# Opening of the first attention: four units split ahead of the first products, one unit later than before in steps 1 and 2

## What is computed

```python
x = x + tanh(g_xattn[0]) * L0_xattn(layernorm(x), ctx, ctx)   # windowed attention, 16 heads of 16
x = x + tanh(g_ffn[0])   * L0_ffn(layernorm(x), ...)          # top-1 of 16 experts
x = x + tanh(g_xattn[1]) * L1_xattn(layernorm(x), ctx, ctx, mask, wq, wk, wv, ...)  # linear attention
x = x + tanh(g_ffn[1])   * L1_ffn(layernorm(x), ...)          # top-2 of 8 experts
```

## Time and profile before

| what | us |
|---|---|
| median of 3 runs (778.89 to 784.18) | 779.85 |
| the profiled execution, its own time | 787.87 |
| its span in the profile | 786.1 |

### The profile page before, as it was taken

The page is one execution under the profiler, slowest core; times in us unless marked ns, Lnnn a source line. Parts: engine busy times, 40 slices in busy tenths (PEclk is TensorE's granted clock), DMA queues, the critical chain, the costliest instruction groups (busy, mean ns, idle before and its releaser), DMA issues. The chain is left out here.

```text
span 786.1 us, 16260 instructions
## 1 busy us (share of the span) xinstructions
PE 717.5 (91%) x5287; PEld 593.2 (75%) x5287; DVE 372.7 (47%) x1131; ACT 315.2 (40%) x851; POOL 344.2 (44%) x468
## 2 busy tenths in 40 slices
PE   4868999998999999998899976999999999999994
PEld 2435766676666999997666643999999999999994
DVE  3366777887546755444888756122122112212210
ACT  3314666665545333331566520432332233233221
POOL 5123333342116556433378623544554454455322
PEclk9977999999989999999999987999999999999998
DMA  4965666666675999933344447257452442445211
GB/s 142 215 126 105 123 123 123 129 119 123 193 250 188 375 373 374 362 103 123 44 75 62 122 134 255 62 153 220 121 140 52 115 109 47 111 110 152 44 23 15
DMA packets 146935, 114.68 MB, mean 146 GB/s; under 512 B 50561, under 2 KB 138284, under 8 KB 146858
## 3 DMA queue, kind: packets, MB, share of 16 engines
q1 hardware_dynamic: 136586, 100.59, 47.0%
q0 software_dynamic: 10272, 13.13, 7.9%
HBM read 153.02 MB, written 24.40 MB: 226 GB/s over the span
## 5 line engine op out<-in xcount | busy, mean ns | idle before, releaser
L1118 ACT ACTIVATE e_hT<-e_HP,e_col 128x128 f32<-128x128 f32 x312 | 88.8, 368 | 184.4 <-PE e_HP L1082 180.0
L1082 PEld LDWEIGHTS e_HP<-e_rT,w_up 128*128 128x128 f32 x1248 | 146.8, 194 | 2.5 <-DVE e_rT L1130 0.6
L1082 PE MATMUL e_HP<-e_rT,w_up 128*128 128x128 f32 x1248 | 147.2, 277 | 0.3 <-DVE e_rT L1130 0.3
L1094 PE MATMUL e_Y<-w_down,e_hT 128*128 128x256 f32 x624 | 141.0, 379 | 0.0
L1094 PEld LDWEIGHTS e_Y<-w_down,e_hT 128*128 128x128 f32 x624 | 115.6, 190 | 14.1
L1140 DVE TENSOR_TENSOR e_yo<-e_Y,e_b2b 128x256 f32<-128x256 f32 x39 | 16.6, 425 | 220.6 <-PE e_Y L1094 220.6
L1175 POOL DMA_INDIRECT out<-e_yo,d_table x39 | 62.9, 1613 | 127.2 <-DVE e_yo L1143 116.1
L429 DVE TENSOR_REDUCE a_nm<-S 128x2 f32<-128x512 f32 x128 | 83.6, 684 | 42.7 <-PE S L529 42.2
L332 ACT ACTIVATE a_pexp<-S 128x1024 f32<-128x1024 f32 x64 | 64.8, 1016 | 35.8 <-PE S L547 35.4
L527 PE MATMUL S<-a_k,a_q 96*128 96x256 bf16 x256 | 54.0, 286 | 9.4 <-DMA a_k<-scr 5.4
L900 PEld LDWEIGHTS e_HP<-e_rT,w_up 128*128 128x128 f32 x512 | 59.5, 192 | 2.2 <-DVE e_rT L956 1.5
(11 more groups left out here) (339 smaller groups left out, 1211.4 us busy)
## 6 DMA issues: line engine op xcount, KB each, us to landing
w_up<-L_ffn_w_in SPq DMA_DIRECT2D x39, 1024.0 KB
w_down<-L_ffn_w_in SPq DMA_DIRECT2D x39, 1024.0 KB
w_up<-L_ffn_W_in SPq DMA_DIRECT2D x16, 1024.0 KB, 9.6
w_down<-L_ffn_W_in SPq DMA_DIRECT2D x16, 1024.0 KB, 11.8
e_b2b<-L_ffn_b_in SPq DMA_DIRECT2D x55, 128.0 KB, 3.5
scr<-a_parts SPq DMA_DIRECT2D x51, 128.0 KB
a_q<-scr SPq DMA_DIRECT2D x17, 192.0 KB, 3.9
a_k<-scr SPq DMA_DIRECT2D x17, 192.0 KB, 4.3
```

What stands on the lines that cost most here:

```text
L1082: i = e.matmul(HP[r][:, j, :], w1[:, n % WR, k, P * j:P * j + P], rT[:, r, k, :], start=(k == 0), stop=(k == 1))
L1094: i = e.matmul(Y[r][:, 0:D], hT[:, r, j, :], w2[:, n % WR, j, :], start=(j == 0), stop=(j == NJ - 1))
L1118: i = e.activation(hT[:, r, j, :], HP[r][:, j, :], ACT.Gelu, bias=col[:, n % 4, j:j + 1])
```

## The change

Units 0 to 3 are prepared in steps -2 and -1 (two in each), none in step 0, unit 4 at the end of step 1, none in step 2; from step 3 on it is unit n+2 again. `SPLIT_AT` says so, `n.splits()` returns it. `scr` gets four buffers. The loads of `x` group 2 and `ctx` group 3 go to the front of SyncE's queue, `x` groups 3 and 4 behind unit 2's reads, `ctx` group 4 behind unit 3's; the later layer's weights (`lin.load`) are issued in step 1, ahead of unit 4's writes. The side tiles are spread 2, 4, 2, 2 instead of 2, 5, 2, 1. `shift` of groups 1 to 4 moves from VectorE (one instruction) to GpSimd (two). The statistics of group 2 move into step -1, those of groups 3 and 4 ahead of the last four maxima of steps 1 and 2. All four memsets of `a_k` are issued before step 0. On ScalarE the maxima of unit 0 and unit 4's first part are copied ahead of the last side tile's product.

```diff
-STATISTICS_AT = {-2: 1, 0: 2, 1: 3, 2: 4}
-PROJECT_AT = {-2: (0, 2), -1: (2, 7), 0: (7, 9), 1: (9, 10)}
+SPLIT_AT = {-2: (0, 1), -1: (2, 3), 0: (), 1: (4,), 2: ()}
+PROJECT_AT = {-2: ((0, 0), (0, 2)), -1: ((2, 4), (4, 6)), 0: (6, 8), 1: (8, 10)}
...
-        scr = nc.dram_tensor("scr", [2, 3, DH, HU, 2, S], BF16, kind="Internal").ap()
+        scr = nc.dram_tensor("scr", [4, 3, DH, HU, 2, S], BF16, kind="Internal").ap()
...
+            load(x_sb, x, 2, s_x)
+            load(ctx_sb, ctx_in, 3, s_cx)
+
+            def write_parts(u):
+                wait(e, s_p3, u.times(2, 2))
+                if u.reg is not None or u.c >= 4:
+                    v = u - 4
+                    wait(e, s_q6[v.mod(4)], v.over4(96, 96))
+                for f in range(3):
+                    e.dma_start(scr[u.mod(4), f].rearrange("d h s t -> h d (s t)"),
+                                parts[:, u.mod(2), 2 * f:2 * f + 2, :].rearrange("p s t -> p (s t)")).then_inc(s_scw[u.mod(2)], 16)
...
-                if n.reg is None and n.c == 0:
-                    load(ctx_sb, ctx_in, 3, s_cx)
-                    for i in range(2, len(GROUPS)):
-                        load(x_sb, x, i, s_x)
-                    load(ctx_sb, ctx_in, 4, s_cx)
-                if n.reg is None and n.c == 2:
-                    lin.load(e)
...
-                u = n + 2
-                if u.prepared():
-                    r = u.mod(2)
-                    wait(e, s_p3, u.times(2, 2))
-                    if u.reg is not None or u.c >= 2:
-                        v = u - 2
-                        wait(e, s_q6[v.mod(4)], v.over4(96, 96))
-                    for f in range(3):
...
+                if n.reg is None and n.c == -2:
+                    write_parts(Unit(0))
+                    write_parts(Unit(1))
+                    read_heads(Unit(0))
+                elif n.reg is None and n.c == -1:
+                    write_parts(Unit(2))
+                    read_heads(Unit(1))
+                    write_parts(Unit(3))
+                    read_heads(Unit(2))
+                    load(x_sb, x, 3, s_x)
+                    load(x_sb, x, 4, s_x)
+                elif n.reg is None and n.c == 0:
+                    read_heads(Unit(3))
+                    load(ctx_sb, ctx_in, 4, s_cx)
+                elif n.reg is None and n.c == 1:
+                    lin.load(e)
+                    write_parts(Unit(4))
+                elif n.reg is None and n.c == 2:
+                    read_heads(Unit(4))
+                else:
+                    for u in n.splits():
+                        write_parts(u)
+                        read_heads(u)
...
+            def shift(g):
+
+                sl = slice(*GROUPS[g])
+                e.wait_ge(s_rs, g + 1)
+                e.tensor_tensor(nmr[:, sl], mv[:, sl, 0], rstd[:, sl], ALU.mult).then_inc(s_mr, 1)
+                e.wait_ge(s_mr, g)
+                e.tensor_scalar(nmr[:, sl], nmr[:, sl], -1.0, None, ALU.mult).then_inc(s_nm, 1)
...
+                first = n.reg is None and n.c < 0
+                if n.reg is None and n.c == -2:
+                    copy_ctx(Unit(1))
+                    split(Unit(0))
+                    rsqrt(1)
+                    shift(1)
+                    split(Unit(1))
+                    e.wait_ge(s_cx[1], 16)
+                    copy_ctx(Unit(2))
                 if n.reg is None and n.c == -1:
-                    e.wait_ge(s_cx[1], 16)
+                    copy_ctx(Unit(3))
+                    split(Unit(2))
+                    split(Unit(3))
+                    rsqrt(2)
+                    shift(2)
                 if n.reg is None and n.c == 1:
-                    for i in range(2, len(GROUPS)):
-                        e.wait_ge(s_cx[i], 16)
-                first = n.reg is None and n.c < 0
-                if first:
-                    copy_ctx(n + 3)
+                    e.wait_ge(s_cx[2], 16)
                 m = n - 1
...
-                if n.reg is None and n.c in STATISTICS_AT:
-                    rsqrt(STATISTICS_AT[n.c])
+                if n.reg is None and n.c in (1, 2):
+                    rsqrt(n.c + 2)
+                    shift(n.c + 2)
+                if n.reg is None and n.c == 1:
+                    split(Unit(4))
+                if n.reg is None and n.c == 2:
+                    e.wait_ge(s_cx[3], 16)
+                    e.wait_ge(s_cx[4], 16)
...
+            def beside(c):
+
+                copy = lambda o, i: e.activation(o, i, ACT.Copy)
+                t = PROJECT_AT[c][0]
+                lin.keep_turned(e, copy, t, turned)
+                lin.keep_product(e, copy, t, product, lin.staged)
+                if c == 1:
+                    e.wait_ge(s_nm, 3)
+                    normalise(Unit(4))
+                lin.keep_turned(e, copy, t + 1, turned)
+                if c == 1:
+                    maxima(Unit(0))
+                    first_parts(Unit(4))
+                lin.keep_product(e, copy, t + 1, product, lin.staged)
+
+            def opening(c):
+
+                copy = lambda o, i: e.activation(o, i, ACT.Copy)
+                if c == -2:
+                    normalise(Unit(1))
+                    first_parts(Unit(0))
+                    first_parts(Unit(1))
+                    lin.keep_turned(e, copy, 0, turned)
+                    e.wait_ge(s_nm, 2)
+                    normalise(Unit(2))
+                    lin.keep_turned(e, copy, 1, turned)
+                    lin.keep_product(e, copy, 0, product, lin.staged)
+                    lin.keep_product(e, copy, 1, product, lin.staged)
+                if c == -1:
+                    first_parts(Unit(2))
+                    normalise(Unit(3))
+                    lin.keep_scalar(e, *PROJECT_AT[c][0], turned, product, lin.staged)
+                    first_parts(Unit(3))
+                    lin.keep_scalar(e, *PROJECT_AT[c][1], turned, product, lin.staged)
...
-                    if n.c == -1:
-                        e.wait_ge(s_nm, 2)
-                    normalise(n + 3)
+                    opening(n.c)
...
-                if n.reg is None and n.c == 0:
-                    normalise(n + 3)
-                if n.reg is None and n.c in PROJECT_AT:
-                    lin.keep_scalar(e, *PROJECT_AT[n.c], turned, product, lin.staged)
...
+                if n.reg is None and n.c in (0, 1):
+                    beside(n.c)
+                elif not first:
+                    for v in n.splits():
+                        first_parts(v)
+                if (n - 1).valid() and not (n.reg is None and n.c == 1):
+                    maxima(n - 1)
...
-                if n.reg is None and n.c in (1, 2):
-                    e.wait_ge(s_nm, 2 * n.c + 1)
-                if u.prepared() and not first and not (n.reg is None and n.c == 0):
+                if n.reg is None and n.c == 2:
+                    e.wait_ge(s_nm, 5)
+                if u.prepared() and not first and not (n.reg is None and n.c in (0, 1)):
                     normalise(n + 3)
...
-                shift(g)
...
-                if u.prepared():
-                    wait(e, s_p1, u.times(1, 1))
...
+                if n.reg is None and n.c == -2:
+                    residual(Unit(0))
+                    statistics(1)
+                    residual(Unit(1))
+                    ones(0)
+                    ones(1)
+                elif n.reg is None and n.c == -1:
+                    residual(Unit(2))
+                    ones(2)
+                    residual(Unit(3))
+                    ones(3)
+                    statistics(2)
+                elif not (n.reg is None and n.c == 1):
+                    for v in n.splits():
+                        residual(v)
                 if n.valid():
...
+                if n.reg is None and n.c in (1, 2):
+                    statistics(n.c + 2)
                 if n.valid():
                     heads(n, 4, 8)
-                if n.reg is None and n.c in STATISTICS_AT:
-                    statistics(STATISTICS_AT[n.c])
-                if n.reg is None and n.c <= 1:
-
-                    e.memset(k6[KR:KM, n.c + 2].rearrange("p h t -> p (h t)").bitcast(F32), BF16_ONES).then_inc(s_ones, 1)
+                if n.reg is None and n.c == 1:
+                    residual(Unit(4))
...
-                    if u == 0 and (n + 2).prepared():
-                        split_transposes(n + 2)
-                    if project is not None and n.c < 0 and u == 0:
-                        lin.project(e, *project, turned, product, s_cx)
+                    if u == (3 if n.reg is None and n.c == 1 else 0):
+                        for i, v in enumerate(n.splits()):
+                            split_transposes(v)
+                            if project is not None and n.c < 0 and project[i][1] > project[i][0]:
+                                lin.project(e, *project[i], turned, product, s_cx)
```

(35 more changed lines are left out.)

57 lines of the change are left out of this document (26 added, 31 removed).

## The result

Runs of both kernels side by side on one chip gave 774.73 us for the changed kernel (median of 12, 770.42 to 779.18) and 782.36 for the kernel before (12 runs, 778.17 to 790.19). The ratio of the means is 0.9894 with a 95% interval of [0.9869, 0.9919]: 8.3 us or 1.1% gained (7.6 by the medians), where 14.6 were forecast. The direction was right, the size was not, and 774.73 us is 0.7 us above the range of 759 to 774. That distance says little by itself: the range was laid from the 779.85 us of the runs first shown, and the kernel before now took 782.36. The failure is in the gain. The profiled execution went from 787.87 to 778.71, its span from 786.1 to 776.9.

The account below looks back on a forecast made before the run. TensorE, underfed in the attention's opening, was taken to bound the kernel. 16.1 us gained by unit 6's transposes, less 1.5 for the clock, made 14.6: 779.85 - 14.6 = 765.2 us, range 759 to 774.

Parts of the forecast that it names:

- What bounds the kernel: TensorE sets the time and is not fed in the attention's opening, 27.4 to 82 us; some 21 us at most to gain.
- Rival C: After the opening, a later wait set by something that did not move loses the gain: about 0, 779 us; chance 0.08.
- The waits that vanish: TensorE's opening waits: 4.0 us for a memset, 3.03 for maxima, 2.6 for the output's normalisation, 1.7 for `ctx` group 3.
- The first product starts at 27.8: End of steps -2 and -1: the attention's first product at 27.8 us instead of 27.42, bounds 27.0 and 30.
- No row shows how long they take; a nearby one is 4.4: Step 2: the 12 KB of maxima take 4.4 us like a read; first `pass2` at 46.3 instead of 55.24.
- the other bound: Step 2: the maxima's DMA takes 6.1 us, the wait behind loads, and lands at 47.9 us.
- The allowance of 1.5 us for the clock: Opening: 1.5 us taken off the 16.1 gained, since remaining waits of 1.65 and 0.9 us might bring a clock fall.
- rival A: Opening: late maxima or group 3 statistics idle TensorE 2 us, the clock falls and loses 3.5; together 5.5, 770.7 us; chance 0.2.
- three signs of being wrong: First product after 30 us; TensorE waiting over 2 us at first `pass2`; attention ending 16 us earlier but the kernel not.
- Unit 6's transposes at 65.8 instead of 81.87: End of the opening: unit 6's transposes at 65.8 us instead of 81.87, 16.1 us gained, the old order from there.
- Rivals B and D: Opening: B, no gaps or fall, up to 19 us, 761, chance 0.12; D, lower clock throughout, slower, up to 797, chance 0.05.

Follow-up runs that it names:

- statistics_moved: Kernel before with early memsets, `shift` on GpSimd and statistics of groups 3 and 4 ahead of the last four maxima, units not prepared earlier: ratio 0.9952.
- statistics_last: Changed kernel with statistics and `shift` (on VectorE) of groups 3 and 4 back at the end of steps 1 and 2: ratio 0.9947.
- memsets_early: Kernel before with only the four memsets of `a_k` moved into steps -2 and -1: ratio 0.9944.
- ctx_weights_late: Changed kernel with both the `ctx` group 4 load behind the maxima in step 1 and the later layer's weights in step 2: ratio 0.9858.
- tight: Changed kernel with side tile 0 turned between units 0 and 1, and ScalarE copying each turned tile ahead of the next parts: 774.29 us, ratio 0.9876.
- ctx_late: Changed kernel with the load of `ctx` group 4 moved from step 0 into step 1, behind unit 0's maxima: ratio 0.9870, run again 0.9846.
- weights_late: Changed kernel with the later layer's weights issued in step 2 instead of step 1: 781.83 us, ratio 0.9881.
- after_again: The changed kernel run once more without any edit, for the spread of one profile: ratio 0.9863 to the kernel before.
- tight_ctx_late: Changed kernel with the reordered steps -2 and -1 and also the `ctx` group 4 load behind the maxima: ratio 0.9847.

## Why the prediction was right or wrong

**What bounds the kernel** was right. TensorE's feeding in the opening was the place, and the remainder did not move by more than two executions of the same kernel differ: from the last transposes to the end it is 569.3 and 574.2 us in the two profiles of before, 570.8, 570.4 and 569.9 after. Rival C (lost later) holds for no more than about 1 us: from unit 6's transposes to the last ones it is 134.9 and 135.1 before, 136.0, 136.5 and 135.9 after. In that stretch TensorE waits 5.4 and 5.3 us for the reads into `a_k` before, and 7.3, 6.6 and 7.0 after; why they land later stays open.

**The waits that vanish** were right, one by one: memset, `ctx`, normalisation, and the 3.03 us for maxima. The runs add that the parts alone do not do it. statistics_moved shows the change's order on VectorE, without the earlier units, worth 4 us, and statistics_last shows the reverse side.

**"The first product starts at 27.8"** was the first wrong step, by 2.2 us, and in two parts. The layout itself held nearly everywhere: unit 1's transposes at 10.36 (forecast 10.25), the first multiply at 12.89 (12.4), an idle of 1.61 ahead of tiles 2 and 3 (1.65), and the 0.86 ahead of tile 5's turn at 26.32 (0.9 in the forecast's list of waits). The 0.5 at the first multiply and some 0.1 to 0.2 at each later handoff make 0.8 us. The other 1.5 are the slow multiplies. I let the first two pass from 12.4 to 16.7, in 4.3 us, though the row that I read had 5.33; they took 5.77. In all fourteen profiles the first product stands at a fixed distance behind the listed time of these two: 22.1 us with the old order (27.42 - 5.33, 27.71 - 5.61, 26.41 - 4.31 in memsets_early), 24.3 with the changed kernel's (30.03 - 5.77, 28.64 - 4.39, 29.73 - 5.47, and 30.02 - 5.74 in ctx_weights_late), 21.5 in both tight versions. So the two more units cost 2.2 us here. The forecast's layout had 1.4 (27.8 - 4.3 against 22.1), and its 0.4 came of setting 4.3 for these multiplies in one kernel beside 5.33 in the other. The rest, up to 1.4 us, is when the first multiplies change their rate (last section), which differs between executions of one kernel. tight takes these 2.2 out and 0.6 more; it meets the late load of `x` group 3 instead, and its profile still gains, since the maxima then have 7.3 us and are not waited for.

**"No row shows how long they take; a nearby one is 4.4"** was the step that cost most. The forecast had 4.4 us for this term, and so no wait for it. The maxima took 6.3 us, near the other bound's 6.1, because of the load ahead of them; they were also issued at 44.21, not 41.8, and the late first product is 2.2 of these 2.4 us. By the queue rule of the Trainium skill (DMA: Bandwidth & Descriptors, Queues, rings and completion order) they stand behind `ctx` group 4; ctx_late fits that rule, with 1.83 us of waiting gone, and in weights_late moving what comes behind changed nothing (1.90 us). With the load out of the way, unit 6's transposes stand 0.8 us from the forecast's 65.8 even though the first product is still 1.8 us late. The step where I chose between two ends took the lower one against a rule that spoke for the upper.

**The allowance of 1.5 us for the clock** was near for this wait: a gap of 1.83 us was followed by 0.50 for 2 us and 0.80 to 0.85 beside it. Taking out the wait (1.8) together with the fall gave 3.4, so the fall cost some 1.6. In after_again the same fall was longer: by the clock of each 2 us from 48 to 56 it lost some 3.4 us, which is rival A's own price, against 1.7 in the profiled execution. This is rival A in place and mechanism, though cheaper than its 5.5 us (4.3 at unit 6's transposes) and it came on top of a late first product. Of the forecast's three signs of being wrong, the first product after 30 was met once (30.03, 28.64, 29.73), the wait of over 2 us at the first `pass2` never (1.83, 1.96, 1.90), and the third not at all.

**The baseline** was the other error. "Unit 6's transposes at 65.8 instead of 81.87" was subtracted from a single execution. In a second one the lower clock behind the first wait was some 3 us shorter, and behind the third there was none. The account at unit 6's transposes: 16.1 forecast, ahead of the 1.5 taken off for the clock; minus 4.3 (70.1 instead of 65.8) is 11.8, what the two first profiles show; minus 2.3, since the mean of the two openings of before is 79.6; minus some 1 us up to the last transposes: 8.5. Measured: 8.3. The 2.3 rests on two executions that are 4.5 us apart, so that the sum comes out this well is partly luck. The rule of the Trainium skill (TensorE: Matmul & The Clock Gate, The HAM clock gate) that the phase of the clock differs from run to run fits the two profiles of before (0.50 and 1.00 from 72 to 74 us). I used it for the changed kernel alone, where it applied as much to the rows I subtracted from.

**Rivals B and D** did not come about. ctx_late is nearest to B: clock 1.00 over 27.4 to 70 us, and unit 6's transposes at 66.6, 0.8 us from the forecast's 65.8. On the mean of before (79.6) that is 13.0 us, not 16.

## What to carry to other kernels

Price a small transfer that is waited for by what was issued ahead of it: here 6.3 us with a 512 KB load in front, at most 4.3 without. Try the large load behind it first, and if its time is unknown with queued traffic in front, take the upper bound. Read a stretch with gaps and clock falls in two executions before subtracting from it; one execution's milestones there were 4.5 us apart here. When several waits stand in a row on different engines, expect each edit alone to expose the next limit (memsets, then operand reads; first product, then a load), and price the set, not the parts.

## What was unexpected of the hardware

- The same wait with and without a fall: 2.63 us for the normalisation went with 0.50 for 4 us and more in one execution of before, and with 1.00 throughout in the next and in statistics_last. In the changed kernel 1.83 us was followed by a fall, and in tight_ctx_late 1.45 us was (0.50 from 44 to 46). The prediction drew a boundary between 1.7 and 2.6 us from the earlier trace rows; these runs show none.
- The first two multiplies after the start are listed with 5.33 and 5.61 us in two executions of the kernel before, and with 5.77, 4.39 and 5.47 in three of the changed kernel, where two later ones take 3.60. The profile gives a granted clock of 1.00 there, but their single matmuls run at two rates. Two of the eight, in the changed kernel as first profiled:

```profile
12.89 1.06 PE L1682 MATMUL S<-c_wkv,c_ctxT 128*128 128x512 f32 x1
17.64 0.59 PE L1682 MATMUL S<-c_wkv,c_ctxT 128*128 128x512 f32 x1
```

  At first they start 0.85 us apart, later 0.43, a factor of two as between the two levels of the clock. The switch came in the sixth matmul here and in the second in after_again; that accounts for the spread of 1.4 us, which moves the first product. The profile's column does not show it.
- With the reads of unit 3 in the queue, one DMA took 1.57 us to issue on SyncE instead of some 0.6, and the last 64 KB reads landed 7.3 and 8.6 us after their issue, where the median of before was 4.4 for 128 KB:

```profile
a_q<-scr SPq DMA_DIRECT2D x1, 64.0 KB, 7.3
a_k<-scr SPq DMA_DIRECT2D x1, 64.0 KB, 8.6
```
